# Causal bias of the plain scores added on VectorE in layer 0, and the product with v for eight heads at once

## The chip, the cores and the metric

The kernel runs on one core of a Trainium2 chip. The metric is the device time of one launch in microseconds (us); the median of three runs is given. Engines are called by the profile's names: PE (TensorE), PEld (its weight loads), DVE (VectorE), ACT (ScalarE), POOL (GpSimd), SP (SyncE, which issues most DMAs).

## What is computed

Two transformer layers over x of 16 batches x 256 tokens x 256 features in fp32, 16 heads of 16 features. Layer 0 has causal attention and gates; layer 1 has full attention with a key mask. Cut to what matters:

```python
# layer 0
scores = einsum('bhqd,bhkd->bhqk', q, k) * scale
scores = where(causal, scores, -inf)
attn = softmax(scores, axis=-1)
out = einsum('bhqk,bhkd->bhqd', attn, v)
x = x + gate_a * (out @ Wproj + bproj);  x = x + gate_m * mlp(adaln(x))
# layer 1: the same without the causal mask (a key mask instead) and without the gates
```

## The kernel before

**Tiling.** Tokens lie on 128 partitions, so a batch has two tiles. Each layer's attention is a software pipeline over batches: step t handles five batches at once. n = t is normalised and transposed, a = t-1 is projected to q, k and v, b = t-2 gets its plain scores, c = t-3 its transposed scores, exponentials and first products with v, and d = t-4 the rest of these and its output projection. An MLP stage follows each layer's attention, in chunks of two batches; nothing of the change lies in it.

**Slots.** A step has 16 slots s, one for each head. Every engine runs its own instructions in program order, and all of them are written out in the order of the slots. In each slot PE does the plain scores of head s of b (`scores`: queries on partitions, into one of three banks `s_bank`) and the transposed scores of one head of c or d (`scoresT`: keys on partitions, into one of two banks `st_bank`), four slots behind (`LAG`). The other work of PE sits in fixed slots (`SLOT`): projection of q in s0 and s1, the transposes of the row maxima in s1, k in s3 and s5, v in s6 and s7, transposes of the attention's output (`oT`, L687) in s8 and s9, transposes of the normalised output (`attnT`, L695) in s11, transposes of the next input (`xT`, L649) in s12, output projection in s14 and s15. The product with v (`attend`, L629) is made for four heads at once, one on each 32 columns of the array, in slots 9, 13, 1 and 5 (`PV_SLOT`).

**Softmax.** It needs the maximum of each query's row. DVE reduces each head's plain scores (L1095 in layer 0, L1099 in layer 1) as soon as PE has made them, and `wait(pe, max_done, ...)` holds the next scores of the same bank until this is done. After 16 heads DVE negates the maxima and splits them in a high and a low part (L1152, L1154; in layer 0 two columns of maxima are joined first, L1149). In the next step's s1 PE transposes them (L657), ACT copies them to `negmaxT` (L839), and SP moves them with two DMAs (L418) into two rows of `q_stack`. Only then may `scoresT` of head 0 run, in s4 (`max_loaded`): its product then yields score minus maximum, and ACT takes the exponential into `probs` (L807), a ring of eight heads.

**Causal bias.** In layer 0 a bf16 product of a triangle of -1e30 with the identity is added in PSUM, for the plain scores (L592) and for the transposed ones (L611).

**Helpers of the chain.** q and k are split in high and low parts: ACT writes the high part from PSUM (`high`, L820 or L824), DVE the low one (`low`, L1055 or L1059), and SP copies both to `q_stack` and `k_stack` (L406). In s8 and s9 DVE takes the reciprocal of the sums and multiplies (L1120, L1122), after the scores' reduction of the same slot; PE's transposes of s11 wait for both (`attn_ready`). ACT makes the modulated input from the transposes of s12 (L873, feature half 0 in s12, half 1 in s13), POOL its low part (L1271), and the q projection of the next s0 waits for it (`xmT_ready`). ACT's copy of the product with v (`outputs`, L814) comes last in the slot of that product.

Of the kernel before, what the change touches and what calls it, by code (L numbers as in the profile page):

```python
# [28 lines left out]
H, HD = 16, 16  # L29
# [6 lines left out]
GROUP = 4  # L36
NG = H // GROUP
SLOTS = H // 2
# [8 lines left out]
PV_SLOT = [(LAG + 5 + GROUP * i) % H for i in range(NG)]  # L47
# [67 lines left out]
def build(nc, x_in, cond_in, mask_in, wa_in, w1_in, w2_in, ada0_in, ada1_in, cols_in, rows_in, ident_in,  # L115
# [4 lines left out]
    with ExitStack() as ctx:  # L120
        def sb(name, shape, dt=fp32):
            return ctx.enter_context(nc.sbuf_tensor(name, shape, dt))
# [15 lines left out]
        tri16 = sb("tri16", [P, P], bf16)  # L138
        table = [sb(f"table{l}", [P, len(KINDS) * NF * B]) for l in range(LAYERS)]
# [3 lines left out]
        probs = sb("probs", [P, 8, 512])  # L143
# [8 lines left out]
        maxima = sb("maxima", [P, 2, 3, H])  # L152
        negmax = sb("negmax", [P, 2, NT, 2, H], f32r)
        negmaxT = sb("negmaxT", [32, T], f32r)
        o_sb = sb("o_sb", [P, 2, NG, T])
# [24 lines left out]
        tri = in_probs(P)  # L180
# [88 lines left out]
        max_joined = sem("max_joined")  # L269
# [227 lines left out]
        def _(pe):  # L497
# [71 lines left out]
            def scores(layer, g, h):  # L569
# [17 lines left out]
                if layer == 0:  # L587
# [30 lines left out]
            def attend(layer, g, r):  # L618
# [6 lines left out]
                for kt in range(NT):  # L625
                    for j in range(GROUP):
                        h = GROUP * r + j
                        lo = first if kt else 0
                        last = mm(o_bank[32 * j:32 * j + 32, lo:T], v_sb[:, g.mod(VBUFS), kt, h, :],  # L629
                                  probs[:, h % 8, kt * T:kt * T + T - lo], start=(kt == 0), stop=(kt == NT - 1),  # L630
                                  tile_position=(0, 32 * j), skip_group_check=True)
                last.then_inc(pv_done, 1)

            def step(layer, t):
                n, a, b, c, d = (t - k for k in range(5))
                gn, ga, gb, gc, gd = (in_layer(layer, s) for s in (n, a, b, c, d))
                for s in range(H):
# [43 lines left out]
                    if s in SLOT["oT"] and d.within(B):  # L681
# [4 lines left out]
                        for r in range(NG):  # L686
# [23 lines left out]
                    if s in PV_SLOT:  # L710
                        r = PV_SLOT.index(s)
                        g, on = (gc, c) if LAG + 5 + GROUP * r < H else (gd, d)
# [79 lines left out]
        def _(act):  # L792
# [6 lines left out]
            def step(layer, t):  # L799
# [3 lines left out]
                def exponentials(g, h):  # L803
                    act.wait_ge(st_ready, g.count(H, h + 1))
                    wait(act, pv_done, g.count(NG, h // GROUP - 1))
                    n = 3 * P if layer == 0 else 4 * P
                    activation(probs[:, h % 8, 0:n], st_bank[h % 2][:, 0:n], ACT.Exp, scale=SCALE)\  # L807
                        .then_inc(exp_done, 1)

                def outputs(g, r):  # L810
# [3 lines left out]
                    activation(o_sb[:, g.mod(2), r, :], o_bank[:, 0:T], ACT.Copy).then_inc(o_copied, 1)  # L814
# [567 lines left out]
```

## Time and profile before

| | us |
|---|---|
| median of three runs | 1178.01 (1175.23 to 1180.79) |
| profiled execution, its own time | 1178.39 |
| its span, first to last instruction | 1176.2 |
| PE busy | 1091.0, 93% of the span |
| DVE, ACT, POOL busy | 752.3 (64%), 622.6 (53%), 252.9 (22%) |
| layer 0's attention, about | 45 to 397 |
| layer 1's attention, about | 620 to 972 |

A span's row gives a start and a duration. The chain of work that ended last is followed back from the last instruction: at each step to what released it. Durations of PE include about 0.17 us in which the array empties, and the next matmul starts before that, so the chain's pieces, which are cut at the ends, are PE's real pace. PE's granted clock was at its upper level, 2.4 GHz, in both attention stages' middle.

### The profile page before, as it was taken

What the parts mean: (1) busy time and instruction counts of PE and PEld (TensorE: products, weight loads), DVE (VectorE), ACT (ScalarE), POOL (GpSimd) and SP (SyncE); (2) the same over time, 40 slices, a digit from 0 to 9 for tenths busy, and PEclk for the clock granted to TensorE, in tenths of its full rate; (3) what the DMA queues carried; (4) which work ended last, traced back from release to release, by engine and by line L of the source; (5) the groups of instructions that cost most, each with busy time, mean ns of one, the idle gap of its engine ahead of it and who ended that gap; (6) DMA issues with size and microseconds to landing.
All of it is one profiled execution on the core that took longest, in us unless ns stands there. A gap on an engine that the chain in (4) does not pass through costs nothing.

```text
span 1176.2 us, 24117 instructions
## 1 busy us (share of the span) xinstructions
PE 1091.0 (93%) x9228; PEld 958.2 (81%) x9228; DVE 752.3 (64%) x1627; ACT 622.6 (53%) x1255; POOL 252.9 (22%) x252
## 2 busy tenths in 40 slices
PE   3989999999999788999985899999999987999998
PEld 3778989998987577899874788888888766988997
DVE  5456666666665457765645687878787646566653
ACT  1146666666665643443331677777777666334431
POOL 5101221211211244223321112121212013121111
PEclk9789999999999999999987899999999999999999
DMA  7547767567561010000057473746456400000001
GB/s 214 114 70 118 129 114 119 97 110 124 135 101 23 7 55 10 13 10 11 14 85 159 72 96 64 97 65 96 70 91 77 58 2 1 19 33 22 19 19 36
DMA packets 50826, 81.49 MB, mean 69 GB/s; under 512 B 8916, under 2 KB 23476, under 8 KB 49620
## 3 DMA queue, kind: packets, MB, share of 16 engines
q1 hardware_dynamic: 49752, 78.37, 37.5%
q10 hardware_dynamic: 960, 1.57, 1.2%
q8 instruction: 74, 1.21, 0.5%
q14 instruction: 40, 0.33, 0.1%
HBM read 22.64 MB, written 8.44 MB: 26 GB/s over the span
## 4 chain that ended last, share of the span: by engine, by line
PE 83%; DVE 4%; DMA 4%; SPq 3%; ACT 2%; issue 2%; POOL 2%; ACTq 1%; POOLq 0%; DVEq 0%
PE g_bank L541 14%; PE st_bank L541 13%; PE o_bank L629 9%; PE o_bank L541 8%; PE s_bank L541 7%; PE s_bank L596 6%; PE st_bank L615 5%; PE s_bank L590 3%; PE st_bank L609 3%; PE st_bank L611 3%; PE s_bank L592 2%; PE g_bank L687 2%; SPq L406 2%; DMA k_stack<-qk_split 2%; DMA q_stack<-negmaxT 1%
## 5 line engine op out<-in xcount | busy, mean ns | idle before, releaser
L807 ACT ACTIVATE probs<-st_bank 128x384 f32<-128x384 f32 (+1 forms) x512 | 273.6, 548 | 156.5 <-PE st_bank L611 89.9
L910 ACT ACTIVATE probs<-st_bank,cols 128x512 f32<-128x512 f32 x128 | 88.0, 689 | 217.6 <-PE st_bank L541 191.1
L541 PE MATMUL st_bank<-qk_split,q_stack 128*128 128x512 f32 x768 | 187.3, 402 | 15.4 <-ACT probs L910 10.8
L1099 DVE TENSOR_REDUCE maxima<-s_bank 128x2 f32<-128x512 f32 x256 | 168.9, 685 | 42.5 <-PE s_bank L596 41.6
L541 PEld LDWEIGHTS st_bank<-qk_split,q_stack 128*128 128x128 f32 x768 | 144.8, 191 | 53.0 <-ACT probs L910 13.8
L1095 DVE TENSOR_REDUCE maxima<-s_bank 128x3 f32<-128x384 f32 x256 | 138.7, 554 | 60.1 <-PE s_bank L592 56.9
L596 PE MATMUL s_bank<-k_stack,q_stack 97*128 97x256 f32 x512 | 115.9, 309 | 17.8 <-DMA k_stack<-mask_dram 10.6
L541 PE MATMUL g_bank<-xmT,wa 128*128 128x256 f32 x768 | 122.7, 299 | 4.8 <-POOL xmT L1271 4.8
L629 PE MATMUL o_bank<-probs,v_sb 128*32 128x256 f32 (+1 forms) x2048 | 124.7, 361 | 1.6 <-ACT probs L807 1.6
L596 PEld LDWEIGHTS s_bank<-k_stack,q_stack 97*128 97x128 f32 x512 | 80.1, 195 | 44.4 <-issue 28.0
L1271 POOL TENSOR_TENSOR xmT<-xm_full,xmT 128x512 fp32r<-128x512 f32 x32 | 42.3, 1322 | 331.8 <-ACT xmT L873 331.8
L541 PEld LDWEIGHTS g_bank<-xmT,wa 128*128 128x128 f32 x768 | 105.0, 199 | 5.7 <-issue 5.2
L615 PE MATMUL st_bank<-q_stack,k_stack 99*128 99x256 f32 x512 | 104.0, 287 | 4.2 <-DMA q_stack<-negmaxT 3.8
L609 PE MATMUL st_bank<-q_stack,k_stack 99*128 99x256 f32 x256 | 93.1, 365 | 4.0 <-DMA q_stack<-negmaxT 3.7
L1199 DVE TENSOR_TENSOR wm_f32r<-probs,k_stack 128x512 fp32r<-128x512 f32 x128 | 92.6, 724 | 4.4
L541 PE MATMUL s_bank<-q_stack,k_stack 128*128 128x256 f32 x512 | 95.3, 284 | 0.0
L541 PE MATMUL o_bank<-q_stack,k_stack 128*128 128x256 f32 x512 | 94.7, 283 | 0.0
L590 PE MATMUL s_bank<-k_stack,q_stack 97*128 97x256 f32 x256 | 88.7, 347 | 6.5 <-DMA k_stack<-qk_split 5.4
L629 PEld LDWEIGHTS o_bank<-probs,v_sb 128*32 128x32 f32 x2048 | 53.8, 110 | 42.8 <-issue 6.1
L615 PEld LDWEIGHTS st_bank<-q_stack,k_stack 99*128 99x128 f32 x512 | 80.0, 193 | 7.7 <-DMA q_stack<-negmaxT 4.4
L541 PEld LDWEIGHTS s_bank<-q_stack,k_stack 128*128 128x128 f32 x512 | 81.6, 192 | 0.0
L541 PEld LDWEIGHTS o_bank<-q_stack,k_stack 128*128 128x128 f32 x512 | 80.0, 189 | 0.0
(114 smaller groups left out, 2104.7 us busy)
## 6 DMA issues: line engine op xcount, KB each, us to landing
q_stack<-qk_split SPq DMA_DIRECT2D x192, 128.0 KB, 4.5
k_stack<-qk_split SPq DMA_DIRECT2D x180, 128.0 KB, 6.0
gate_rows<-gate_dram SPq DMA_DIRECT2D x32, 128.0 KB, 3.4
w_dram<-w_in SPq DMA_DIRECT2D x8, 512.0 KB, 7.2
wm_f32r<-w_dram SPq DMA_DIRECT2D x4, 1024.0 KB, 7.9
out<-x_sb SPq DMA_DIRECT2D x8, 512.0 KB, 2.9
x_sb<-x_in SPq DMA_DIRECT2D x4, 512.0 KB, 7.8
k_stack<-qk_split ACTq DMA_DIRECT2D x12, 128.0 KB, 8.7
```

The source lines that it names most:

```text
L541: last = mm(dst, weights[i], rows[j], start=(f == 0 and n == 0), stop=(f == tiles - 1 and n == len(TERMS) - 1))
L590: mm(bank[:, P:3 * P], q[:, P:T], k, start=True, stop=False)
L596: last = mm(bank[:, i * T:(i + 1) * T], q[:, i * P:(i + 1) * P], k, start=True, stop=True)
L609: mm(bank[:, 0:T], k[:, 0:P], q, start=True, stop=False)
L615: last = mm(bank[:, i * T:(i + 1) * T], k[:, i * P:(i + 1) * P], q, start=True, stop=True)
L629: last = mm(o_bank[32 * j:32 * j + 32, lo:T], v_sb[:, g.mod(VBUFS), kt, h, :], probs[:, h % 8, kt * T:kt * T + T - lo], start=(kt == 0), s ...
L807: activation(probs[:, h % 8, 0:n], st_bank[h % 2][:, 0:n], ACT.Exp, scale=SCALE)\
L910: activation(h_full[:, m % 2], st_bank[m % 2][:, :], ACT.Gelu, bias=cols[:, cb + m:cb + m + 1])\
L1095: v.reduce_max(maxima[:, gb.mod(2), 0:3, slot], bank[:, 0:3 * P].rearrange("p (i n) -> p i n", n=P), AX.X)\
L1099: v.reduce_max(maxima[:, gb.mod(2), 0:2, slot], bank[:].rearrange("p (i n) -> p i n", n=T), AX.X).then_inc(max_done, 1)
L1199: v.tensor_tensor(hT[1][:, :, m], h, hT[0][:, :, m], ALU.subtract).then_inc(m_hT, 1)
L1271: g_.tensor_tensor(xmT[:, gn.mod(2), 1], xm_full[:], xmT[:, gn.mod(2), 0], ALU.subtract)\
```

## The change

1. **Causal bias, layer 0.** The bf16 product of L592 goes. DVE's one reduction of 3 x 128 columns is replaced by two `tensor_tensor_reduce`: scores plus bias, written back to the bank, with the running maximum as a second result, over the 128 keys of query tile 0 and the 256 keys of tile 1. The bias comes from `tri_wide`, a tile of 128 columns of zeros and the triangle. Each is two instructions on DVE, the second of which reads the running maximum out. The join of two columns of maxima (L1149) goes. The wait for PE becomes an instruction of its own (`wait_apart`). Layer 1's reduction stays.
2. **Product with v, both layers.** `GROUP` goes from 4 to 8: one `attend` takes eight heads, as two quads in the two halves of `o_bank`, and one ACT copy of 512 columns takes the place of two of 256. `PV_SLOT` becomes slots 12 and 4.
3. **Ring.** `probs` holds twelve heads instead of eight.
4. The scratch for dynamic DMAs falls from 4096 to 256.

```diff
-GROUP = 4
+LOWEST = -3.0e38
+GROUP = 8
 NG = H // GROUP
+QUAD = 4
+NQ = H // QUAD
+RING = 12
-PV_SLOT = [(LAG + 5 + GROUP * i) % H for i in range(NG)]
+PV_SLOT = [(LAG + GROUP * (i + 1)) % H for i in range(NG)]
-        probs = sb("probs", [P, 8, 512])
+        probs = sb("probs", [P, RING, 512])
+        def ring(g, h):
+            return (g.const * H + h) % RING
 # PE, scores
                     mm(bank[:, P:3 * P], q[:, P:T], k, start=True, stop=False)
-                    mm(bank[:, 0:P], q[:, 0:P], k[:, 0:P], start=False, stop=False)
-                    last = mm(diagonal(bank), ident16[:], tri16[:].unsqueeze(1).to_broadcast((P, 2, P)),
-                              start=False, stop=True)
+                    last = mm(bank[:, 0:P], q[:, 0:P], k[:, 0:P], start=False, stop=True)
 # PE, attend
-                for kt in range(NT):
-                    for j in range(GROUP):
-                        h = GROUP * r + j
+                for u in range(GROUP // QUAD):
+                    for kt in range(NT):
+                        for j in range(QUAD):
+                            h = GROUP * r + QUAD * u + j
 # ACT, exponentials and outputs
-                    wait(act, pv_done, g.count(NG, h // GROUP - 1))
+                    wait(act, pv_done, g.count(NG, (h - RING) // GROUP + 1))
-                    activation(o_sb[:, g.mod(2), r, :], o_bank[:, 0:T], ACT.Copy).then_inc(o_copied, 1)
+                    activation(o_sb[:, g.mod(2), 2 * r:2 * r + 2],
+                               o_bank[:].rearrange("p (u n) -> p u n", u=GROUP // QUAD), ACT.Copy).then_inc(o_copied, 1)
 # DVE, the maxima of layer 0
-                            v.reduce_max(maxima[:, gb.mod(2), 0:3, slot],
-                                         bank[:, 0:3 * P].rearrange("p (i n) -> p i n", n=P), AX.X)\
-                                .then_inc(max_done, 1)
+                            for i in range(NT):
+                                keys = slice(i * P, (2 * i + 1) * P)
+                                last = v.tensor_tensor_reduce(
+                                    out=bank[:, keys], in0=bank[:, keys], in1=tri_wide[:, T - (i + 1) * P:T],
+                                    scale=1.0, scalar=LOWEST, op0=ALU.add, op1=ALU.max,
+                                    accum_out=maxima[:, gb.mod(2), i, slot:slot + 1])
+                            last.then_inc(max_done, 1)
```

**PE in layer 1, from the maxima's transposes (s1) to the first transposed scores that need them (s4), before:**

```order
L657 MATMUL g_bank0<-ident,negmax 32x128 x2
L541 MATMUL g_bank1<-xmT,wa 128x256 x6
L629 MATMUL o_bank<-probs,v_sb 32x256 x8
L596 MATMUL s_bank2<-k_stack,q_stack 128x256 x2
L615 MATMUL st_bank0<-q_stack,k_stack 128x256 x2
L596 MATMUL s_bank0<-k_stack,q_stack 128x256 x2
L615 MATMUL st_bank1<-q_stack,k_stack 128x256 x2
L541 MATMUL g_bank0<-xmT,wa 128x256 x6
L596 MATMUL s_bank1<-k_stack,q_stack 128x256 x2
L615 MATMUL st_bank0<-q_stack,k_stack 128x256 x2
```

and now:

```order
L665 MATMUL g_bank0<-ident,negmax 32x128 x2
L549 MATMUL g_bank1<-xmT,wa 128x256 x6
L602 MATMUL s_bank2<-k_stack,q_stack 128x256 x2
L621 MATMUL st_bank0<-q_stack,k_stack 128x256 x2
L602 MATMUL s_bank0<-k_stack,q_stack 128x256 x2
L621 MATMUL st_bank1<-q_stack,k_stack 128x256 x2
L549 MATMUL g_bank0<-xmT,wa 128x256 x6
L602 MATMUL s_bank1<-k_stack,q_stack 128x256 x2
L621 MATMUL st_bank0<-q_stack,k_stack 128x256 x2
```

One product with v stood between them and now none does; what is left is a half of the q projection, one of the k projection and the scores.

**PE in layer 1, from the first transposes of the output (s8) to those of the normalised output (s11), before:**

```order
L687 MATMUL g_bank0<-ident,o_sb 128x128 x4
L596 MATMUL s_bank0<-k_stack,q_stack 128x256 x2
L615 MATMUL st_bank1<-q_stack,k_stack 128x256 x2
L687 MATMUL g_bank1<-ident,o_sb 128x128 x4
L629 MATMUL o_bank<-probs,v_sb 32x256 x8
L596 MATMUL s_bank1<-k_stack,q_stack 128x256 x2
L615 MATMUL st_bank0<-q_stack,k_stack 128x256 x2
L596 MATMUL s_bank2<-k_stack,q_stack 128x256 x2
L615 MATMUL st_bank1<-q_stack,k_stack 128x256 x2
L695 MATMUL g_bank0<-ident,attn 128x128 x4
```

and now:

```order
L695 MATMUL g_bank0<-ident,o_sb 128x128 x4
L602 MATMUL s_bank0<-k_stack,q_stack 128x256 x2
L621 MATMUL st_bank1<-q_stack,k_stack 128x256 x2
L695 MATMUL g_bank1<-ident,o_sb 128x128 x4
L602 MATMUL s_bank1<-k_stack,q_stack 128x256 x2
L621 MATMUL st_bank0<-q_stack,k_stack 128x256 x2
L602 MATMUL s_bank2<-k_stack,q_stack 128x256 x2
L621 MATMUL st_bank1<-q_stack,k_stack 128x256 x2
L703 MATMUL g_bank0<-ident,attn 128x128 x4
```

The product with v of s9 has left, and so has that of s5, which stood ahead of these rows behind the k projection.

**DVE in layer 0, from the low part of k (s5) on, before:**

```order
L1055 TENSOR_TENSOR qk_split<-g_bank,qk_split 128x512
L1095 TENSOR_REDUCE maxima<-s_bank 128x3 x2
L1045 TENSOR_SCALAR xn<-x_sb,mv,rstd 128x256 x2
L1095 TENSOR_REDUCE maxima<-s_bank 128x3
L1120 RECIPROCAL rsum<-g_bank 128x16
L1122 TENSOR_TENSOR attn<-g_bank,rsum 128x256
```

and now (ISA on maxima alone is the reading out of the running maximum):

```order
L1064 TENSOR_TENSOR qk_split<-g_bank,qk_split 128x512
L1109 ISA s_bank,maxima<-s_bank,tri_wide 128x128
L1109 ISA maxima 128x1
L1109 ISA s_bank,maxima<-s_bank,tri_wide 128x256
L1109 ISA maxima 128x1
L1109 ISA s_bank,maxima<-s_bank,tri_wide 128x128
L1109 ISA maxima 128x1
L1109 ISA s_bank,maxima<-s_bank,tri_wide 128x256
L1109 ISA maxima 128x1
L1054 TENSOR_SCALAR xn<-x_sb,mv,rstd 128x256 x2
```

One instruction for each head has become four, between a low part that waits for ACT and the work of s7 to s9.

On ACT, the copy of the product with v that now stands in s12 comes between the two halves of the modulated input; before, it came behind both, in s13.

## Rows read from the trace of the kernel before

**Rows 1.** Stretch, us, busy us (xcount) of PE, PEld, DVE, ACT, POOL; PE clock, DMA, GB/s.
```profile
150.00:250.00 100.00, 99.65 (x1053) 89.91 (x1055) 67.55 (x156) 63.00 (x135) 19.97 (x22) 1.00 0.69 116
...
700.00:800.00 100.00, 100.00 (x966) 85.34 (x964) 80.32 (x169) 74.93 (x155) 17.41 (x20) 1.00 0.57 81
```

**Rows 2.** Timeline of POOL, layer 0: start us, us, line, tiles, [idle before <-releaser].
```profile
208.69 1.29 POOL L1271 TENSOR_TENSOR xmT<-xm_full,xmT 128x512 fp32r<-128x512 f32 x1 [11.87 <-ACT xmT L873]
...
230.07 1.29 POOL L1271 TENSOR_TENSOR xmT<-xm_full,xmT 128x512 fp32r<-128x512 f32 x1 [11.97 <-ACT xmT L873]
```

**Rows 3.** The chain that ended last, layer 0, 205 to 210: start us, us, what.
```profile
205.21 0.12 PE s_bank L590
205.33 0.06 PE s_bank L591
205.39 0.13 PE s_bank L592
...
206.88 0.79 PE o_bank L629 x16
207.67 0.31 PE s_bank L590
```

**Rows 4.** The chain, layer 1, 739 to 765 us.
```profile
749.88 0.22 PE g_bank L657 x2
...
750.82 1.00 PE o_bank L629 x16
...
753.93 0.25 PE st_bank L615 x2
...
754.66 0.71 PE g_bank L541 x6
...
755.37 1.00 PE o_bank L629 x16
...
762.94 0.44 PE g_bank L695 x4
```

**Rows 5.** Groups of DVE, 150 to 250 us: out<-in, shapes xcount | busy us, mean ns.
```profile
L1055 DVE TENSOR_TENSOR qk_split<-g_bank,qk_split 128x512 fp32r<-128x512 f32 x9 | 6.2, 692 | 10.6 <-ACT qk_split L820 10.6
...
L1122 DVE TENSOR_TENSOR attn<-g_bank,rsum 128x256 f32<-128x256 f32 x10 | 4.3, 425 | 0.3
...
L1039 DVE BATCH_NORM_AGGREGATE mv<-stats 128x2 f32<-128x6 f32 x10 | 1.2, 165 | 0.7
```

**Rows 6.** Timeline of DVE, layer 0 (first row) and layer 1.
```profile
206.49 1.01 DVE L1095 TENSOR_REDUCE maxima<-s_bank 128x3 f32<-128x384 f32 x2
...
756.28 0.88 DVE L1059 SCALAR_TENSOR_TENSOR qk_split<-g_bank,cols,qk_split 128x256 fp32r<-128x256 f32 x2 [0.25 <-ACT qk_split L824]
...
758.04 0.69 DVE L1099 TENSOR_REDUCE maxima<-s_bank 128x2 f32<-128x512 f32 x1 [0.29 <-PE s_bank L596]
...
761.42 0.42 DVE L1122 TENSOR_TENSOR attn<-g_bank,rsum 128x256 f32<-128x256 f32 x1
```

**Rows 7.** Row maxima's DMAs: SP's timeline, landing time over L418, chain after 149 us.
```profile
750.85 1.19 SPq L418 DMA_DIRECT2D q_stack<-negmaxT  x2
...
DMA to landing us min/median/max: 2.1/2.1/3.0
...
149.16 3.00 DMA q_stack<-negmaxT
...
152.20 0.39 PE st_bank L609
```

**Rows 8.** Timeline of ACT, layer 1 and (last row) layer 0.
```profile
745.64 0.61 ACT L873 ACTIVATE xm_full<-g_bank,table 128x256 f32<-128x256 f32 x1
746.09 0.62 ACT L873 ACTIVATE xmT<-g_bank,table 128x256 fp32r<-128x256 f32 x1
...
755.40 0.84 ACT L824 ACTIVATE qk_split<-g_bank,cols 128x256 fp32r<-128x256 f32 x2
...
218.27 0.60 ACT L820 ACTIVATE qk_split<-g_bank 128x512 fp32r<-128x512 f32 x1 [0.22 <-PE g_bank L541]
```

More of the change, by code:

```diff
@@ L624, in attend @@
                 first = P if layer == 0 else 0
-                for kt in range(NT):
-                    for j in range(GROUP):
-                        h = GROUP * r + j
[L628 to L631, printed above, removed]
+                for u in range(GROUP // QUAD):
+                    for kt in range(NT):
+                        for j in range(QUAD):
+                            h = GROUP * r + QUAD * u + j
+                            lo = first if kt else 0
+                            last = mm(o_bank[32 * j:32 * j + 32, u * T + lo:(u + 1) * T],
+                                      v_sb[:, g.mod(VBUFS), kt, h, :],
+                                      probs[:, ring(g, h), kt * T:kt * T + T - lo], start=(kt == 0),
+                                      stop=(kt == NT - 1), tile_position=(0, 32 * j), skip_group_check=True)
                 last.then_inc(pv_done, 1)
@@ L685, in step @@
                         bank = take(layer, t, f"oT{i}")
-                        for r in range(NG):
+                        for r in range(NQ):
                             last = transpose(bank[:, r * P:(r + 1) * P], o_sb[:, gd.mod(2), r, i * P:(i + 1) * P],
@@ L711, in step @@
                         r = PV_SLOT.index(s)
-                        g, on = (gc, c) if LAG + 5 + GROUP * r < H else (gd, d)
+                        g, on = (gc, c) if LAG + GROUP * (r + 1) < H else (gd, d)
                         if on.within(B):
@@ L878, in step @@
                         r = PV_SLOT.index(s)
-                        g, on = (gc, c) if LAG + 5 + GROUP * r < H else (gd, d)
+                        g, on = (gc, c) if LAG + GROUP * (r + 1) < H else (gd, d)
                         if on.within(B):
@@ L1089, in step @@
                             wait(dve, negmax_ready, gb.count(1, -1))
-                        dve.wait_ge(s_ready, gb.count(H, s + 1))
+                        if layer == 0:
+                            wait_apart(dve, s_ready, gb.count(H, s + 1), dve_passed)
+                        else:
+                            dve.wait_ge(s_ready, gb.count(H, s + 1))
                         bank = s_bank[S_BANK[s]]
@@ L1147, in negative_maximum @@
                 dve.wait_ge(max_done, g.count(H, H))
-                if layer == 0:
-                    v.tensor_tensor(m[:, 1], m[:, 1], m[:, 2], ALU.max).then_inc(max_joined, 1)
-                    dve.wait_ge(max_joined, g.count(1, 1))
                 wait(dve, negmaxT_ready, g.count(1, -1))
-                v.tensor_scalar(dst[:, :, 0], m[:, 0:NT], -1.0, None, ALU.mult).then_inc(negmax_hi, 1)
+                v.tensor_scalar(dst[:, :, 0], m, -1.0, None, ALU.mult).then_inc(negmax_hi, 1)
                 dve.wait_ge(negmax_hi, g.count(1, 1))
-                v.scalar_tensor_tensor(out=dst[:, :, 1], in0=m[:, 0:NT], scalar=-1.0, in1=dst[:, :, 0],
+                v.scalar_tensor_tensor(out=dst[:, :, 1], in0=m, scalar=-1.0, in1=dst[:, :, 0],
                                        op0=ALU.mult, op1=ALU.subtract).then_inc(negmax_ready, 1)
```

18 lines of the change are left out of this document (10 added, 8 removed).

## The prediction

> **What bounds the kernel now.** First the busy time by stretch: in the middle of both attention stages PE is busy for 99.65 and 100.00 of 100 us at its upper clock, 2.4 GHz (granted 1.00), while DVE stands at 67.55 and 80.32, ACT at 63.00 and 74.93 [rows 1]. Then the rhythm: POOL's xmT comes once a step, and in layer 0 two of them start 21.38 us apart [rows 2]. Then the chain of waits: it holds PE's pieces and nothing else in these stretches. So what leaves PE is won, unless a wait that PE's own work has covered comes to light; the question is how much cover goes along. The chain's pieces give PE's pace in layer 0: 0.12, 0.06 and 0.13 us for a head's plain scores, as much for its transposed ones, and 0.79 for a product with v, plus 0.19 by which the next piece is longer than usual (0.31 against 0.12) [rows 3]. In layer 1 a product takes 1.00, six matmuls of a projection 0.71, four transposes 0.44 [rows 4]. The sum of a step of layer 0 is 16 x 0.62 + 8 x 0.71 + 4 x 0.44 + 0.15 + 4 x 0.98 = 21.4, as measured: no cover is short now.
>
> **Products for eight heads.** A product of layer 1 has 128 more columns in the second key tile and costs 1.19 against 0.98 [rows 3, 4]: 0.21 for 128 columns of four matmuls side by side. Columns thus make 0.63 in layer 0 and 0.84 in layer 1, and 0.35 is left in each for starting and ending. The 0.19 of it behind the product surely goes with the product; the rest may in part be seams between quads, of which there are as many as before. I take 0.32 for each of 64 products that go: -20.5 us, with 12 and 22 as ends.
>
> **L592 goes.** The chain gives it 0.13 [rows 3], 256 times: 33 us. But the next weights are fp32, and L591's 128 columns are short. L591 takes 0.06 when bf16 weights follow; the four transposes, 128 columns and fp32 weights each, take 0.44, 0.11 each [rows 4]. If an fp32 load of 128 columns wants 0.11, then L591 and L592, 0.19 together, become 0.11: I take 0.08 a head, -20.5 us, with 13 and 33 as ends, since the transposes are nearest in shape. The Trainium skill, "TensorE: Matmul & The Clock Gate", section "LDWEIGHTS (loading the stationary operand)", puts a load at columns / 1.2 ns, 107 ns for 128; by it the gain would be 0.08 a head as well, and by the chain's row alone 0.13, -33 us.
>
> **Maxima with the bias, DVE, layer 0.** No row shows this form. A two-input operation of 256 columns out of PSUM takes 0.425, one of 512 0.692 [rows 5], so 128 would take 0.29. Two reductions span 1.01, each 0.55 long, so the second starts 0.10 before the first ends [rows 6]. The reading out is bounded by the shortest row, 0.165 [rows 5]. A head then holds DVE for 0.65 (all overlapped) to 1.05 (nothing overlapped), against 0.455. I take 0.84: the operations at full length, since each reading needs its end, the readings overlapped. Of the 0.54 that a reduction holds it today that is 16 x 0.3 = 5 us more in a step, and with 67.55% of 21.38 [rows 1, 2] 14.4 + 5 = 19.4 of some 22: DVE does not become the bound, but it gets later. The separate wait instruction I cost at nothing: when DVE is late, it has long been satisfied.
>
> **Three covers that go.** The products leave s1, s5, s9 and s13 for s4 and s12. Lateness of others was hidden behind them.
>
> *First, s1 to s4: the maxima's DMAs.* In layer 1 PE ends the transposes at 749.88 + 0.22 = 750.10 and needs the rows at 753.93 [rows 4]: cover 3.83. SP issues the first DMA at 750.85, the second 0.60 later, which lands 2.1 after that, and PE needs some 0.31 to start again (DMA's end 152.16; the piece then takes 0.39, not 0.12) [rows 7]: 0.75 + 0.60 + 2.1 + 0.31 = 3.76. Only 0.07 is spare, and the product with its 1.19 goes: a wait of 1.12. In layer 0 the cover becomes 0.71 + 2 x 0.54 + 0.71 + 0.23 = 2.73 against about 3.7: 0.95. In each layer's last two steps, where the cover is short already, all 1.2 comes out. Sum: 14 x (0.95 + 1.12) + 4 x 1.2 = +34 us.
>
> *Second, s5 to s11: attn.* The k projection ends at 755.37. ACT's high part starts at 755.40, DVE's low part at 756.28, and behind it in DVE's queue stand two heads' maxima, xn, a head, reciprocal and attn, a head, reciprocal and attn, which ends at 761.42 + 0.42 = 761.84 [rows 4, 6, 8]. That is 6.47 with 0.29 of waiting for scores [rows 6], which come sooner now: 6.18, and 0.31 until PE runs. PE's cover was 762.94 - 755.37 = 7.57 [rows 4]; without two products it is 5.19. Wait in layer 1: 1.30. In layer 0 ACT takes 0.60 for 0.84 [rows 8], the low part 0.13 less, and four reductions of 0.61 become four groups of 0.84: 7.04 against a cover of 6 x 0.54 + 2 x 0.71 + 2 x 0.44 = 5.54: wait 1.50. Behind it are queued the maxima of heads 10 to 15; the long product of s12 lets DVE catch up. Some 12.5 steps a layer have all of it: +35 us, and +3 for the last steps.
>
> *Third, s12 to the next s0: xmT.* ACT's copy now waits for the product's end in s12 and stands ahead of an exponential and xm's second half. From that end: copy 0.56, exponential 0.6, two xm of 0.45 and 0.62, then POOL 1.29 + 0.07 and PE's start 0.31 [rows 2, 8]: 3.9. PE has 0.19 + 0.48 + 2 x 1.19 + 0.48 = 3.5 in layer 1 and 3.75 in layer 0. Waits 0.40 and 0.15, 13 times: +7 us.
>
> These waits lie behind one another on PE, so they add. A step of layer 0 becomes 21.38 - 1.28 - 0.64 + 0.95 + 1.50 + 0.15 = 22.1; one of layer 1 grows by 2.2. The MLP stages stay. Ring and scratch: nothing; twelve slots make no exponential wait for a product (heads 0 to 3 need one of a step ago).
>
> **Sum.** -20.5 - 20.5 + 34 + 35 + 3 + 7 = +38. The profiled execution took 1178.4, its span 1176.2, and the median is 1178.0, so it stands for the runs: 1216. Of this layer 1 has some 31 us and layer 0 some 7. With the ends of all terms taken one at a time: 13 us less if L592 is worth 33, though each head's plain scores on the second cover give 0.05 back (4 in all), 9 less if a group of DVE takes 0.65 (12.5 x 0.76), 10 more at 1.05; 8 more if half of a product's start stays; a fifth of a us in each of the three latencies in both layers is 8 to each side. Together some 1196 to 1234.
>
> **Rivals.** *The covers hold* (faster): if DVE, ACT and SP run ahead once PE has gaps, and the latencies above contain waits for PE itself, PE stays the bound and only the first two terms count: 1178 - 41 = 1137. It needs chains of 5.2 and 2.6 us where the trace shows 6.2 and 3.5; for it speaks only that PE waits nowhere today. It decides as soon as the second chain is under 5.2. *One of the two great covers holds* (half way): 1216 - 35 = 1181, from 1170 to 1192. *DVE at full lengths*: a group costs 1.05, the wait in layer 0 is 2.34 and DVE has 14.4 + 9.6 = 24 us a step, more than PE: the step is DVE's, about 24, 2 x 15 more than forecast: 1245. The rows speak against it with 0.10 of overlap between reductions [rows 6]. The Trainium skill, "VectorE: DVE Perf Modes", section "The DRAIN you can't avoid", says that the next operation does not start until the pipe is empty, which would be this rival; the overlap in the rows speaks against the strict reading, at least for reductions. *Merging does nothing*: if the fixed 0.35 is seams, the product of eight heads costs two of four, and 20.5 comes back: 1236.
>
> **How the numbers follow.** Forecast 0.60, 1216. DVE at full lengths 0.12, merging does nothing 0.08, one great cover holds 0.12, all hold 0.08. A measurement of this kernel can tell 0.5%, about 6 us, from no change. Faster: 0.08 + 0.03; same, 1172 to 1184: 0.05; slower: 0.84. The range leaves out the fast rival, most of the half-way one and the upper part of the DVE rival: 1188 to 1240.
>
> **What would show it.** Right: idle time of PE in front of the transposes of attn, released by DVE, over 1 us in each step; in front of the first transposed scores, released by the DMAs of negmaxT, about 1 us; PE's busy share in the attention stages near 88%; POOL's xmT 22 us apart in both layers (the second stands near 20 now). Wrong: xmT 19.5 apart in layer 0, or DVE busy over 95% there, or a product of eight heads of 2 us in layer 0 instead of 1.6. The forecast falls if a head's group on DVE is far from 0.84, or if DVE does the work behind the low part of k in another rhythm when PE has gaps.

## The result

The changed kernel is slower: 1205.05 us median against 1177.32 for the kernel before, ratio 1.0237 with a 95% interval of 1.0205 to 1.0270. The forecast was 1216 in a range of 1188 to 1240. Its profiled span is 1202.6 us against 1176.2. One execution each of the kernels all_three, two_queues and covered below took 2028 to 2567 us and is left out of their medians; that of two_queues was the one with the profile, so there are no rows for it.

The busy time of the same two stretches as in [rows 1] (stretch, us, then PE, PEld, DVE, ACT, POOL with their counts, PE's granted clock, DMA, GB/s):

```profile
150.00:250.00 100.00, 95.25 (x1007) 86.40 (x1006) 77.98 (x378) 62.75 (x128) 21.13 (x23) 1.00 0.63 120
700.00:800.00 100.00, 90.79 (x874) 78.24 (x874) 75.37 (x154) 66.92 (x131) 15.54 (x18) 1.00 0.45 73
```

PE was busy all the time; now it stands idle for 4.75% in layer 0 and 9.2% in layer 1, at the upper clock in both. DVE, which got new work in layer 0 only, is at 78% there: it did not become the bound. POOL's timeline gives the steps, as [rows 2] did:

```profile
209.50 1.29 POOL L1286 TENSOR_TENSOR xmT<-xm_full,xmT 128x512 fp32r<-128x512 f32 x1 [12.06 <-ACT xmT L882]
...
230.54 1.28 POOL L1286 TENSOR_TENSOR xmT<-xm_full,xmT 128x512 fp32r<-128x512 f32 x1 [12.40 <-ACT xmT L882]
...
753.03 1.29 POOL L1286 TENSOR_TENSOR xmT<-xm_full,xmT 128x512 fp32r<-128x512 f32 x1 [13.23 <-ACT xmT L882]
775.22 1.30 POOL L1286 TENSOR_TENSOR xmT<-xm_full,xmT 128x512 fp32r<-128x512 f32 x1 [13.21 <-ACT xmT L882]
```

A step of layer 0 takes 21.04 instead of 21.38, one of layer 1 22.19 instead of 20.15. By the same timelines, up to layer 0's last xmT the changed kernel is 0.9 us ahead (336.12 against 336.98). It wins 1.3 more to layer 1's first, loses 25.6 in the fifteen steps of layer 1 (336.07 against 310.52) and 3.0 in what follows the last xmT (271.2 against 268.2): together the 26.4 between the spans. So all of the loss lies from layer 1's first xmT on, where only the products with v changed.

Which of PE's instructions waited for whom, in 110 to 340 us (layer 0: first two rows) and in 690 to 905 us (layer 1: last two; us in total, times, the longest):

```profile
PE st_bank L615 <- DMA q_stack<-negmaxT: 8.7, 11, 1.1
PE g_bank L703 <- DVE attn L1138: 2.1, 11, 0.2
...
PE st_bank L621 <- DMA q_stack<-negmaxT: 9.9, 10, 1.6
PE g_bank L703 <- DVE attn L1138: 9.5, 10, 1.0
```

In the kernel before, the same views have one wait of 0.4 us for the maxima's DMA and none for attn. A wait also costs a start, which counts as busy: the first piece behind it is longer than the same piece elsewhere. The chain of waits of layer 1 shows both (start us, us, what):

```profile
747.29 0.66 PE g_bank L703 x4
...
754.27 0.15 issue
754.42 0.95 PE g_bank L549 x6
...
756.38 0.37 ACT negmaxT L848
...
756.83 0.55 SPq L426
...
757.43 2.15 DMA q_stack<-negmaxT
...
759.62 0.50 PE st_bank L621 x2
760.12 1.86 PE o_bank L636 x32
761.99 0.43 PE s_bank L602 x2
```

Four transposes take 0.66 where [rows 4] has 0.44 for four, two transposed scores 0.50 where the rows beside them have 0.24, six matmuls of the q projection 0.95 for 0.71. Three covers (the stretches of PE's own work that run while another engine's chain is under way) are short in a step: attn's at 747.29, xmT's at 754.42, the maxima's DMA at 759.62. And the product for eight heads costs 1.86 + 0.19 = 2.05, against 2 x 1.19 for two of before.

The chain of layer 0 (the same columns):

```profile
205.81 1.44 PE o_bank L636 x32
207.25 0.32 PE s_bank L598
207.57 0.06 PE s_bank L599
207.63 0.17 PE st_bank L615
...
211.01 0.83 PE g_bank L549 x6
...
216.04 0.39 PE st_bank L615
```

A head's plain scores are down to 0.12 + 0.06, but L615, the first piece behind them, is 0.17 (its like took 0.12 before, as L598 still does): the 0.17 is there in bias_only too, and 0.12 again in merge_only, so it comes with L592's going. That its load of fp32 weights then has only the 0.06 of L599 to run beside fits this, but no run isolates the load.

### The profile page after: what moved, and what is told of

The parts are those of the page before. It is cut to its first block, busy times and chain, and to the rows that moved or that the text cites. A ratio compares the mean times of both kernels' runs of the same rounds, so it can differ in the third digit from the quotient of the medians.

```text
span 1202.6 us, 24469 instructions
## 1 busy us (share of the span) xinstructions
PE 1071.4 (89%) x8972; PEld 945.9 (79%) x8972; DVE 789.2 (66%) x2379; ACT 613.8 (51%) x1191; POOL 252.8 (21%) x253
## 4 chain that ended last, share of the span: by engine, by line
PE 63%; DVE 13%; DMA 8%; issue 6%; ACT 5%; SPq 4%; POOL 1%; ACTq 1%; POOLq 0%; DVEq 0%
PE st_bank L549 13%; PE o_bank L636 9%; PE g_bank L549 8%; PE o_bank L549 8%; PE s_bank L549 7%; DMA q_stack<-negmaxT 5%; PE st_bank L621 3%; PE s_bank L602 3%; DVE s_bank L1109 2%; DVE maxima L1115 2%; PE st_bank L615 2%; SPq L414 2%; DVE attn L1138 2%; PE g_bank L703 2%; PE s_bank L598 2%
## 5 line engine op out<-in xcount | busy, mean ns | idle before, releaser
L1109 DVE CUSTOM_DVE_ANT_0 s_bank<-s_bank,tri_wide 128x128 f32<-128x128 f32 (+1 forms) x512 | 169.3, 387 | 45.2 <-PE s_bank L599 44.7
L602 PE MATMUL s_bank<-k_stack,q_stack 97*128 97x256 f32 x512 | 112.5, 302 | 17.9 <-DMA k_stack<-mask_dram 13.5
L621 PE MATMUL st_bank<-q_stack,k_stack 99*128 99x256 f32 x512 | 105.9, 291 | 18.1 <-DMA q_stack<-negmaxT 17.4
L636 PE MATMUL o_bank<-probs,v_sb 128*32 128x256 f32 (+1 forms) x2048 | 113.4, 363 | 1.3 <-ACT probs L815 1.3
L615 PE MATMUL st_bank<-q_stack,k_stack 99*128 99x256 f32 x256 | 87.1, 341 | 15.7 <-DMA q_stack<-negmaxT 15.4
L598 PE MATMUL s_bank<-k_stack,q_stack 97*128 97x256 f32 x256 | 85.5, 335 | 10.9 <-DMA k_stack<-qk_split 7.3
L636 PEld LDWEIGHTS o_bank<-probs,v_sb 128*32 128x32 f32 x2048 | 59.8, 111 | 39.7 <-issue 7.0
```

The source lines that it names most:

```text
L598: mm(bank[:, P:3 * P], q[:, P:T], k, start=True, stop=False)
L602: last = mm(bank[:, i * T:(i + 1) * T], q[:, i * P:(i + 1) * P], k, start=True, stop=True)
L615: mm(bank[:, 0:T], k[:, 0:P], q, start=True, stop=False)
L621: last = mm(bank[:, i * T:(i + 1) * T], k[:, i * P:(i + 1) * P], q, start=True, stop=True)
L636: last = mm(o_bank[32 * j:32 * j + 32, u * T + lo:(u + 1) * T], v_sb[:, g.mod(VBUFS), kt, h, :], probs[:, ring(g, h), kt * T:kt * T + T - ...
L1109: last = v.tensor_tensor_reduce(out=bank[:, keys], in0=bank[:, keys], in1=tri_wide[:, T - (i + 1) * P:T], scale=1.0, scalar=LOWEST, op0=AL ...
```

## Experiments

Twelve kernels. Each ratio is to executions of the kernel before taken beside that kernel's own; their median was 1177.3 beside the changed kernel and 1176.4 to 1179.8 beside the twelve. "Step" is the distance of two xmT in the steady part of a layer, from POOL's timeline.

| kernel | median us | ratio to before (95%) | step, layer 0 | step, layer 1 |
|---|---|---|---|---|
| before | 1177.32 | | 21.38 | 20.15 |
| changed | 1205.05 | 1.0237 (1.0205 to 1.0270) | 21.05 | 22.20 |
| merge_only | 1213.59 | 1.0304 (1.0266 to 1.0343) | 21.49 | 22.19 |
| bias_only | 1165.43 | 0.9893 (0.9854 to 0.9932) | 20.19 | 20.15 |
| late_slots | 1188.65 | 1.0084 (1.0058 to 1.0110) | 20.71 | 21.03 |
| all_three | 1177.96 | 0.9983 (0.9962 to 1.0004) | 20.23 | 20.58 |
| heavy_bias | 1236.26 | 1.0485 (1.0451 to 1.0518) | 22.33, then 23.93 | 22.20 |
| late_k23 | 1169.07 | 0.9916 (0.9892 to 0.9941) | 19.97 | 20.32 |
| two_queues | 1171.76 | 0.9936 (0.9910 to 0.9961) | no rows | no rows |
| two_queues_v | 1178.16 | 0.9988 (0.9972 to 1.0005) | 20.25 | 20.55 |
| xn_late | 1205.95 | 1.0245 (1.0219 to 1.0272) | 21.09 | 21.86 |
| covered | 1167.64 | 0.9915 (0.9885 to 0.9945) | 20.04 | 20.15 |
| covered_early_o | 1174.10 | 0.9979 (0.9961 to 0.9996) | 20.11 | 20.29 |
| covered_early_xn | 1162.13 | 0.9869 (0.9839 to 0.9899) | 19.80 | 19.92 |

**The two halves of the change apart.** merge_only, against the changed kernel:

```
-                    last = mm(bank[:, 0:P], q[:, 0:P], k[:, 0:P], start=False, stop=True)
+                    mm(bank[:, 0:P], q[:, 0:P], k[:, 0:P], start=False, stop=False)
+                    last = mm(diagonal(bank), ident16[:], tri16[:]..., start=False, stop=True)
...
-                                last = v.tensor_tensor_reduce(out=bank[:, keys], ...)
+                            v.reduce_max(maxima[:, gb.mod(2), 0:3, slot], ...)
```

> The changed kernel with the causal bias put back on PE (its matmul and the one reduction of a head on DVE); only the products with v for eight heads, their slots and the ring remain of the change. My theory (what the merge gives on PE, 0.33 us a product, is less than the covers that it takes away): layer 1 is as in the changed kernel, some 30 us longer than before; layer 0 gets -0.64 a step from the merge and +0.8 from the wait for the maxima's DMAs, nothing from attn because each head has 0.08 more work of PE, so about +4 us: 1212 in all, between 1204 and 1220. Rival, that the bias on DVE is what makes the changed kernel slow: then this one is at 1157, 20 us faster than before. Rival, that L592 is worth its whole row of 0.13: then this one is further above the changed kernel, at 1220 or more.

1213.6 where 1212 was expected, and layer 1's step is the changed kernel's. The waits in 110 to 340 us:

```profile
PE st_bank L618 <- DMA q_stack<-negmaxT: 5.3, 11, 0.5
```

With L592's work back on PE the DMA wait of layer 0 is 0.48 a step in place of 0.79, and no wait for attn is among PE's: PE's own work is cover. The rival with the bias as the cause (1157) is out.

bias_only, against the changed kernel:

```
-GROUP = 8
+GROUP = 4
-RING = 12
+RING = 8
-PV_SLOT = [(LAG + GROUP * (i + 1)) % H for i in range(NG)]
+PV_SLOT = [(LAG + 5 + GROUP * i) % H for i in range(NG)]
```

> The changed kernel with the products for four heads, their old slots and the ring of eight; only the bias on DVE and the matmul of the plain scores' bias gone from PE remain of the change. My theory: with four products in s1, s5, s9 and s13 all covers stand, PE stays the bound and gains 0.08 us a head of layer 0, 256 times: 1157, between 1150 and 1165, xmT in layer 0 some 20.1 us apart and in layer 1 20.15 as before. Rival, L592 worth its row of 0.13: 1144. Rival, DVE with the bias becomes late by itself: no gain or a loss, 1172 or more, with waits of PE for attn in layer 0.

Two xmT of layer 0:

```profile
183.08 1.28 POOL L1285 TENSOR_TENSOR xmT<-xm_full,xmT 128x512 fp32r<-128x512 f32 x1 [11.12 <-ACT xmT L881]
203.28 1.29 POOL L1285 TENSOR_TENSOR xmT<-xm_full,xmT 128x512 fp32r<-128x512 f32 x1 [10.63 <-ACT xmT L881]
```

The step is 20.19, 1.19 less than before: 0.074 a head for L592, near the 0.08 of the prediction and far from its row of 0.13. The median, 1165.4, lies above the expected 1157 and just outside its range. The first four steps of layer 0 gain nothing (86.6 us against 86.1), and the stretch between the layers, from layer 0's last xmT to layer 1's first, is 3.0 us longer than before. That stretch goes with PE's granted clock (the columns of [rows 1]; before, bias_only, late_k23):

```profile
336.98:597.47 260.49, 242.27 (x1775) 212.79 (x1774) 160.56 (x338) 119.02 (x230) 78.17 (x68) 0.99 0.11 23
324.51:588.04 263.53, 246.87 (x1740) 216.34 (x1740) 165.32 (x435) 118.89 (x230) 78.13 (x68) 0.95 0.10 23
321.35:587.01 265.66, 248.09 (x1746) 217.02 (x1746) 165.58 (x437) 117.95 (x223) 78.21 (x68) 0.94 0.10 23
```

Over all the kernels with rows it takes 259.2 to 260.9 us where the clock is 0.98 or 0.99 in its mean, 260.0 and 262.8 at 0.97, and 263.3 to 266.3 at 0.94 to 0.96. In the first four steps of layer 0 the clock is 0.86 before and 0.82 in bias_only. So part of what these kernels win in the steady steps is missing again in stretches where the clock is lower than before. That the clock is the cause fits the numbers and is not tested, and why it is lower there no run shows.

Together: alone the bias takes 1.19 off a step of layer 0, but on top of the merge only 21.49 - 21.05 = 0.44. What it takes off PE is paid back as waiting once a cover is short.

**Giving covers back.** late_slots:

```
-PV_SLOT = [(LAG + GROUP * (i + 1)) % H for i in range(NG)]
+PV_SLOT = [(LAG + 1 + GROUP * (i + 1)) % H for i in range(NG)]
...
-                        g, on = (gc, c) if LAG + GROUP * (r + 1) < H else (gd, d)
+                        g, on = (gc, c) if LAG + 1 + GROUP * (r + 1) < H else (gd, d)
```

> The changed kernel with its two products one step-part later, in s13 and s5 instead of s12 and s4. The product in s5 then stands behind the k projection and so inside the cover of attn, and the copy of the product in s13 stands behind both halves of xm. My theory: waits for attn and for xmT go, the wait for the maxima's DMAs (0.95 us in layer 0, 1.2 in layer 1) stays: layer 0 some 15 us under before, layer 1 some 10 us over it: about 1172, between 1162 and 1182. Rival, one common cause for both waits of PE (ACT or DVE late as a whole): the waits move elsewhere and the time stays at 1195 to 1210.

In 690 to 905 us:

```profile
PE st_bank L621 <- DMA q_stack<-negmaxT: 10.3, 11, 1.2
...
PE g_bank L703 <- DVE attn L1138: 1.6, 10, 0.2
```

16.4 us under the changed kernel, so the waits did not move elsewhere; the DMA's stays, as the theory has it. But 1188.7 is not 1172 and lies outside its range. Each steady step is 0.3 longer than expected, which is about 8 us; 4.2 more are the stretch between the layers (264.7 us, clock 0.96) and 3.1 what follows the last xmT (271.3 against 268.2). The waits show a remainder for attn, in layer 1 0.16 and a start of 0.2 in each step, for which the theory had no term. It is still there with the long chain well covered (below).

all_three has late_slots' edit and these:

```
-SLOT = {"q": (0, 1), "negmaxT": 1, "k": (3, 5), ...
+SLOT = {"q": (0, 1), "negmaxT": 1, "k": (2, 3), ...
...
-                    for e in range(2):
-                        sp.dma_start(q_stack[ROW_MAX + e:ROW_MAX + e + 1, ...], negmaxT[H * e:H * (e + 1)])
+                    sp.dma_start(q_stack[ROW_MAX:ROW_MAX + 2, ...], negmaxT[:])
```

> The changed kernel with three edits: products in s13 and s5, the k projection in s2 and s3 instead of s3 and s5 (0.71 us more work of PE ahead of the first transposed scores, and the end of k earlier), and the maxima's two rows sent by one DMA instead of two (0.6 us less in the chain to the first transposed scores). My theory: all three covers hold again, and only PE's two gains are left, 20.5 us for 64 products and 20.5 for the plain scores' bias: about 1138, between 1130 and 1152, PE busy for nearly all of both attention stages. Rival, the latencies contain waits for PE itself and new waits come in the places of the old: 1165 or more. Rival, the merge as such gives nothing (its fixed part is seams between quads): 1158.

1178.0: the expectation failed by 40 us, and the time is that of its first rival, that new waits come in the places of the old. But these waits are not new, they are the old ones that did not go: in layer 1 PE waits 0.46 a step for the DMA and 0.16 for attn, which with two starts of 0.26 and 0.2 are the 1.08 by which 20.58 is above PE's own work, 20.15 - 0.66 = 19.5. A part of the first is in the chain of layer 1:

```profile
743.77 3.01 DMA q_stack<-negmaxT
```

One DMA of 32 KB lands 3.01 us after its issue; the two of 16 KB had 0.55 + 2.15 = 2.70. The edit meant to shorten the chain made it 0.3 longer. late_k23 is all_three with the two DMAs again:

> Products in s13 and s5 and the k projection in s2 and s3, with the maxima's rows sent by two DMAs again. With one DMA for both rows its landing took 3.01 us, against 0.55 of issue and 2.15 of landing for two: one DMA was 0.3 us longer, not 0.6 shorter. So my theory says 0.3 us a step less than with one DMA, in both layers: xmT about 19.95 apart in layer 0 and 20.3 in layer 1, 1169 in all, between 1163 and 1175. Rival (the wait is set by something else that PE needs there, an exponential or the copy): 1178 as with one DMA.

1169.07 for 1169, steps of 19.97 and 20.32 for 19.95 and 20.3: by the steps this term is understood. That the whole time came out to 0.1 us is in part luck, since the stretch between the layers is 2.8 us longer than in all_three. two_queues lets ACT send the second row:

```
+                        act.wait_ge(negmaxT_copied, gc.count(1, 1))
+                        act.dma_start(q_stack[ROW_MAX + 1:ROW_MAX + 2, ...], negmaxT[H:2 * H]).then_inc(max_loaded[...], 16)
```

> As the run before it here, but the second of the maxima's rows is sent by ACT right behind its own copy and the first by SP, so that neither DMA waits for the other's issue. My theory: the chain to the first transposed scores is 0.55 us shorter once more, the wait for these rows is gone in layer 0 and nearly in layer 1, ACT pays 0.5 us in a step, for which it has the room (67% busy): xmT 19.75 apart in layer 0 and 20.0 in layer 1, about 1163, between 1155 and 1170. Rival: the issue on ACT makes the exponentials of heads 14 and 15 late and gives back what it brings: 1169 or more.

1171.8, the rival's time; whether for the rival's reason is not shown. two_queues_v also has `"v": (4, 6), "oT": (7, 8)`:

> As the run before it here, and the v projection in s4 and s6 instead of s6 and s7, the transposes of o in s7 and s8 instead of s8 and s9, so that the chain through DVE to attn in s11 has a head's work more of cover. My theory: the last wait of PE for attn (0.2 to 0.3 us) goes, and PE's own work sets the step: 19.5 in both layers, 1153, between 1145 and 1162. Rival: DVE's order moves the wait, since the low part of k, xn and the two attn now stand closer together and the reductions behind them come late: 1163 or more.

Its DMA issues (queue, count, KB, median us from issue to landing), and PE's loads in 110 to 340 us:

```profile
q_stack<-negmaxT ACTq DMA_DIRECT2D x32, 16.0 KB, 2.1
q_stack<-negmaxT SPq DMA_DIRECT2D x32, 16.0 KB, 2.7
...
PEld s_bank L597 <- DVE maxima L1111: 7.2, 35, 0.3
```

Issued at the same time from two engines, one lands after 2.1 us and the other after 2.7: no earlier than one behind the other from SP. So little is won there, and PE's loads for plain scores wait for the reductions of DVE 35 times (in late_k23 13 times). This is what the rival of this run said, that xn, both attn and the reductions then follow closely on DVE, and 1178.2 is its time (1163 or more), not the theory's 1153.

**The size of a head's group on DVE.** heavy_bias, against the changed kernel:

```
+                            v.reduce_max(maxima[:, gb.mod(2), NT, slot:slot + 1], bank[:, P:3 * P], AX.X)
                             for i in range(NT):
```

> The changed kernel with one more reduction over 256 columns of each head of layer 0 ahead of the two biased ones, its result unused: a head's group on DVE goes from the 0.62 us measured in the changed kernel (0.84 was forecast) to about 0.95. It measures what the size of that group is worth. My theory (four groups stand in the chain to attn, and its cover in layer 0 is nearly used up): the wait for attn grows from some 0.3 us to 1.6, layer 0's steps from 21.05 to about 22.3, DVE at some 97% there, 19 us in all over the changed kernel: 1224, between 1218 and 1235; layer 1 stays at 22.2. Rival (DVE has time to spare in layer 0, its share was 78%, and the size of a group is hidden): 1205 as in the changed kernel.

The first steps take 22.33, 1.28 more than in the changed kernel: four groups of 0.32 in the chain to attn, as expected. The last five of layer 0 take 23.93, which is 8 of the 12 us by which 1236 lies above 1224; the stretch between the layers, 7.1 us longer than in the changed kernel at a clock of 0.96 against 0.99, has the rest. The price of the group is read from the steps ahead of these five. The clock there (windows, columns as above):

```profile
322.00:329.40 7.40, 6.08 (x55) 5.81 (x53) 6.81 (x32) 4.23 (x9) 0.00 (x0) 1.00 0.94 137
...
330.40:334.10 3.70, 3.70 (x40) 2.22 (x38) 2.36 (x11) 1.79 (x4) 0.00 (x0) 0.56 0.95 297
```

and the chain behind the wait for attn:

```profile
329.39 0.66 PE g_bank L703 x4
...
330.78 0.85 PE g_bank L657 x4
331.63 2.44 PE o_bank L636 x32
```

In these steps the granted clock falls a microsecond after PE starts again, to 0.56 in the mean of the next 3.7 us, which is mostly the lower level, 1.2 GHz; the pieces are up to twice as long (0.85 for 0.44, 2.44 for 1.44), and the step pays 1.6 us. PE had been idle for 1.32 us before it, and for 1.32 us as well at the same place of the earlier steps, whose clock stayed at 1.00. What tips it is not shown.

**Which part of the chain to attn counts.** xn_late, against the changed kernel:

```
-                    if s == 7 and n.within(B):
+                    if s == 10 and n.within(B):
                         row_normalise(layer, n)
```

> The changed kernel with DVE's two operations of xn moved from the seventh head of a step to the tenth, behind both attn and not ahead of them; nothing else. They take 0.66 us in layer 1 and 0.59 in layer 0 and stand in the chain from the k projection to attn. My theory (PE waits for attn because the chain through DVE is longer than its cover): the wait goes from 1.2 us to some 0.55 in layer 1 and from some 0.3 to nothing in layer 0: steps of 21.6 and 20.8, about 1192 in all, between 1187 and 1198. Rival (DVE's last operations there wait for PE's transposes of o anyway, and the work ahead of them is hidden): 1202 to 1208.

1205.95, the rival's time. In 690 to 905 us:

```profile
PE g_bank L703 <- DVE attn L1138: 3.0, 10, 0.3
...
PEld g_bank L657 <- DVE xn L1054: 3.1, 10, 0.3
```

PE's wait for attn did fall, from 0.95 to 0.30, the 0.66 of xn: the rival's reason is wrong though its time is right. A wait for xn with its start (0.21) came behind it, and 0.34 of a step is left of the gain in layer 1, -0.04 in layer 0. Over the whole execution even that does not show, since the stretch between the layers is 4.4 us longer than in the changed kernel, at a clock of 0.96 against 0.99.

**Is there a version that beats both?** covered has late_slots' edit, k in s2 and s3, xn at the tenth head and `"v": (3, 7)`:

> Products in s13 and s5, the k projection in s2 and s3, xn of DVE at the tenth head, and the first half of the v projection in s3 behind k, 0.71 us more of PE's work ahead of the first transposed scores. My theory: no cover is short, PE's own pieces set the step: 19.5 in layer 0 and 19.5 in layer 1, about 1150, between 1144 and 1160. Rival (v ahead of its time makes PE wait for the low part of q, which has the same bank, or DVE's two attn stay behind their short last cover): 1163 or more.

The chain of layer 1:

```profile
746.69 0.26 DVE rsum L1136
...
747.32 0.69 DVE maxima L1115
748.00 0.65 DVE xn L1054 x2
...
748.70 0.65 PE g_bank L657 x4
```

Nothing waits for the maxima's DMA any more in layer 1, yet the step is 20.15: waits for attn (0.16) and for xn, and two starts, are left. 1167.6 instead of 1150 is the rival's time (1163 or more), and the second of its two reasons, DVE's attn behind their short last cover, is among these waits. covered_early_o also has `"v": (3, 6), "oT": (7, 8)`:

> As the run before it here, but v's second half in s6 and the transposes of o in s7 and s8 instead of s8 and s9: from the last transposes of o to those of attn PE then has two and a half heads of its own work, and DVE needs a head's maxima, a reciprocal and attn. My theory: it takes away what is left of the wait for attn, if anything is: 19.5 in both layers, 1148, between 1142 and 1158. Rival: the copy of the product of s5 (0.9 us on ACT, behind an exponential) comes too late for s7, 1158 or more.

1174.1 and steps of 20.11 and 20.29. PE's wait for attn is gone from the table of waits; that for xn took its place (0.4 and a start), since xn is now behind both attn and two heads' reductions in a shorter stretch. Neither the theory nor the rival (a late copy) said this. The last run puts xn ahead of both attn again, one head earlier than in the changed kernel:

```
-                    if s == 10 and n.within(B):
+                    if s == 6 and n.within(B):
```

> As the run called covered, but DVE's two operations of xn at the sixth head instead of the tenth (the changed kernel has them at the seventh). In late_k23 DVE is idle for 0.51 us in layer 1 between the reductions of the sixth and the seventh head, and rstd has been there for 1.6 us by then. At the tenth head they made PE wait for xn (0.3 us and a start of 0.2). My theory: neither the chain to attn nor the one to xn is longer than its cover, so the two waits that covered has left (0.37 and 0.36 us with their starts) both go: 19.6 in both layers, against 20.0 and 20.15, 1155 in all, between 1148 and 1163, faster than both kernels and than the bias alone. Rival (the last two reciprocals and attn of DVE have only the cover from the second transposes of o, which no move of xn changes): the wait for attn stays, 19.9 in layer 1 and 19.8 in layer 0, about 1162.

The chain of layer 1:

```profile
744.70 0.40 DVE maxima L1115
745.11 0.11 issue
745.21 0.69 DVE maxima L1115
...
747.32 0.43 DVE attn L1138
...
747.80 0.66 PE g_bank L703 x4
```

1162.1, 19.80 and 19.92: the rival's numbers. The wait for xn is gone and that for attn stays, 2.5 us in ten steps of layer 1. Its chain is a short one: at 745.11 DVE has nothing to do and waits for the plain scores of s8, which PE ends at 745.01. From 745.21 on it has their reduction, a reciprocal and attn, the reduction of s9, a reciprocal and attn, 747.75 - 745.21 = 2.54 us. With the 0.20 ahead of it and 0.27 until PE runs at its pace that is 3.01. PE's work over it is two transposes of o (0.44 each) and 3.5 heads of 0.48, 2.56: 0.45 is missing. The wait survives late_slots, late_k23 and this run, which differ in what stands ahead of s8, and it vanished where the transposes of o stand one head earlier (covered_early_o, two_queues_v). This version takes 1.3% less time than before (0.9869, 0.9839 to 0.9899) and 3.6% less than the changed kernel by the medians; against bias_only (0.9893, 0.9854 to 0.9932) the intervals overlap, so it is not shown that the merge brings anything over the bias alone. By steps it does: layer 1, where the merge is all that differs from before in PE's work, takes 19.92 against 20.15, with 0.45 still lost to attn, and layer 0 takes 19.80 against bias_only's 20.19.

## Why the prediction was right, and where not

*The two gains.* The merge: 0.79 + 0.19 twice against 1.44 + 0.20 in layer 0, and 1.19 twice against 2.05 in layer 1, is 0.32 and 0.33 a product; 0.32 was forecast. The rival that the fixed part is seams between quads is out: nearly all of the 0.35 is paid once a product, whether it has one quad or two. The Trainium skill, "TensorEngine Tiling (Array Packing)", section "Key Properties", says that changing the tiling mode drains TensorE; the rows fit this, with some 0.35 for the change there and back, though no run here separates the change of mode from other costs of starting and ending a product. L592: 0.074 a head by bias_only's steps, 0.08 forecast; the rest of its 0.13 now shows as L615's 0.17 for 0.12.

*The first cover.* Forecast waits with their start 0.95 and 1.12; measured 0.79 + 0.22 = 1.01 in layer 0 and 0.99 + 0.26 = 1.25 in layer 1. Right.

*The second cover.* Layer 1: 1.30 forecast, 0.95 + 0.22 = 1.17 measured. Layer 0: 1.50 forecast, 0.19 + 0.22 = 0.41 measured, so the sign "over 1 us in each step" did not come there, and its xmT came 21.04 and not 22 apart. Here is the step that failed: "I take 0.84: the operations at full length, since each reading needs its end". DVE's timeline of the changed kernel:

```profile
199.73 0.29 DVE L1109 CUSTOM_DVE_ANT_0 s_bank<-s_bank,tri_wide 128x128 f32<-128x128 f32 x1
199.94 0.14 DVE L1109 DVE_READ_ACCUMULATOR2_ANT maxima<- 128x1 f32 x1
199.94 0.47 DVE L1109 CUSTOM_DVE_ANT_0 s_bank<-s_bank,tri_wide 128x256 f32<-128x256 f32 x1
200.32 0.14 DVE L1109 DVE_READ_ACCUMULATOR2_ANT maxima<- 128x1 f32 x1
200.32 0.33 DVE L1109 CUSTOM_DVE_ANT_0 s_bank<-s_bank,tri_wide 128x128 f32<-128x128 f32 x1
```

The reading starts 0.21 and 0.38 after its operation, before the 0.29 and 0.47 of that are over, and at the same moment as the next operation, so it adds nothing that the rows show (no run has the operation without its reading). The next head starts 0.59 after this one; where heads follow one another it is 0.59 to 0.63. That is the prediction's own value for "all overlapped", 0.65, or a little under it: its range had the right end, and its choice was the wrong one. With 0.62 the prediction's own formula gives 3.68 + 4 x 0.62 - 5.54 = 0.62 instead of 1.50, 11 us in layer 0's 13 steps, about the distance of 1216 from 1205 (0.41 was measured, 0.2 less again). heavy_bias shows that the term itself stands: 0.32 more a head, 1.28 more a step. The section "Two Vector instructions with no wait between them" of the Trainium skill's page "VectorE: DVE Perf Modes" counts an operation with an accumulator as two instructions and holds the next only in listed cases; this trace agrees with it, since none of these operations waits for the one in front to end, and disagrees with the strict reading of "The DRAIN you can't avoid", the section that the prediction weighed.

*The third cover.* 0.40 and 0.15 forecast; in the rows 0.15 + 0.24 = 0.39 in layer 1 and 0.83 - 0.71 = 0.12 in layer 0. Right.

*The sum.* 21.38 - 1.28 - 0.64 + 1.01 + 0.41 + 0.12 = 21.00 for the measured 21.05, and 20.15 - 0.66 + 1.25 + 1.17 + 0.39 = 22.30 for 22.20. What follows layer 1's last xmT, 3.0 us, was in the sum with the short covers of each layer's end. By layers the sum was less good than as a whole: some 7 us for layer 0 and 31 for layer 1 were forecast, and up to layer 0's last xmT the kernel is 0.9 us faster, from layer 1's first on 28.6 slower. PE's busy share was forecast near 88% in both stages: 91 in layer 1, 95 in layer 0.

*What the runs add.* The prediction took the chain to attn as one, from the k projection on. late_slots and covered_early_xn show a second, short one inside it, from the plain scores of s8, which stays when the long one is covered. It is one reason why a version with every named cover restored gained 15 us over before and not the 41 of the two first terms: in the steady steps it takes about 10 of the missing 26. The first four steps of each layer gain next to nothing (86.7 us against 86.1, and 88.1 against 88.9), and the stretch between the layers is 3.0 longer, both at a lower granted clock than before (0.82, 0.83 and 0.96 against 0.86, 0.85 and 0.99); what lowers it there stays open.

## What to carry on

Where an engine is busy all the time, its work is also the cover of every chain that runs beside it: before taking work out or putting it together, write down for each wait how long the chain is and how much work lies over it, and price the removal by the spare. Price a wait with the start behind it (here 0.21 to 0.26 us), and look for the next shorter chain inside the one that you relieve: four of the reliefs tried here brought up another wait. If an operation of two instructions has no row, let the overlap that neighbouring rows show (0.46 from start to start for reductions 0.55 long) decide between the ends, and test the term with one heavier copy.

## What the runs showed of the hardware

- Reading out an accumulator of DVE takes 0.14 us and starts together with the next operation, so it runs beside it. A pair of 128 and 256 columns with a bias and a maximum takes 0.62 us from head to head; a reduction of 384 columns took 0.46 from start to start (two in 1.01, each 0.55, [rows 6]).
- A DMA of 32 KB to two rows landed after 3.01 us, one of 16 KB after 2.15 (2.1 in the median and 3.0 at most before, [rows 7]). The Trainium skill, "DMA: Bandwidth & Descriptors", section "Anatomy of one DMA — SWDGE (gpsimd) path", gives 2.0 us fixed and bytes by 436 GB/s for DMAs issued from GpSimd, by which 16 KB more would be, as an estimate, 0.04 us; here, issued from SP and to two rows of one tile, they were 0.86.
- Two DMAs of 16 KB issued at once from two queues landed after 2.1 and 2.7 us, in all as late as one after the other.
- PE's granted clock fell to 0.56 for 3.7 us behind an idle time of 1.32 us in the last five steps of heavy_bias, and stayed at 1.00 behind the same idle time in the steps before.
- Between the layers PE's granted clock was 0.99 in the mean before and 0.94 to 0.99 in the other kernels, and that stretch took 259.2 to 260.9 us at 0.98 or above and 263.3 to 266.3 at 0.96 or below.
